# Expert attention in a six-stage decoder: gathered tokens laid out by position, square root on ScalarE, residual by matmul, scores on all partitions

## The reference

```python
probs  = softmax(h @ Wg)                                  # 16 experts
idx    = sort(top_k(probs.T, cap))                        # 2 tokens of each 32 per expert
hg     = h gathered at idx
q, k, v = hg @ Wq[e] + bq, hg @ Wk[e] + bk, hg @ Wv[e] + bv   # 64 features
p      = softmax(q @ k.T / 8, axis=1)                     # over the queries' axis
ao     = (p @ v) @ Wo[e] + bo
y      = h + scatter_add(ao at idx)
yn     = layer_norm(y) * ln_g + ln_b
out    = layer_norm(h + yn)                               # the decoder's own norm
```

## Time and profile before

| what | value |
| --- | --- |
| median of 3 runs | 3803.97 us (3803.84 to 3806.27) |
| profiled execution | 3800.63 us, span 3797.80 us |
| mean granted TensorE clock | 0.95 |
| busy: TensorE, VectorE, ScalarE, GpSimd | 3290, 3118, 2817, 2568 us |

### The profile page before, as it was taken

The page is one execution under the profiler, slowest core; times in us unless marked ns, Lnnn a source line. Parts: engine busy times, 40 slices in busy tenths (PEclk is TensorE's granted clock), DMA queues, the critical chain, the costliest instruction groups (busy, mean ns, idle before and its releaser), DMA issues. The chain is left out here.

```text
span 3797.8 us, 75246 instructions
## 1 busy us (share of the span) xinstructions
PE 3290.3 (87%) x23328; PEld 2494.5 (66%) x23360; DVE 3118.3 (82%) x5163; ACT 2817.2 (74%) x5141; POOL 2567.5 (68%) x2971
## 2 busy tenths in 40 slices
PE   8996988979963688999988989898899879997887
PEld 5664666668542477777767777777777757775565
DVE  5665999955386699999899989989999849998887
ACT  2222777854475799899898998989899737776887
POOL 1222767730086599888888988898898936665676
PEclk9998999979976899999999999999999989998999
DMA  2112222242213111121111211111111112322111
GB/s 61 55 55 56 44 53 49 50 106 46 52 34 85 37 52 57 50 54 53 54 53 56 57 50 57 49 53 56 55 52 51 48 47 68 77 54 64 51 61 45
DMA packets 285549, 209.62 MB, mean 55 GB/s; under 512 B 131416, under 2 KB 249752, under 8 KB 285224
## 3 DMA queue, kind: packets, MB, share of 16 engines
q1 hardware_dynamic: 285224, 205.72, 19.9%
HBM read 149.18 MB, written 51.41 MB: 53 GB/s over the span
## 5 line engine op out<-in xcount | busy, mean ns | idle before, releaser
L2896 POOL TENSOR_TENSOR ma_ch<-ma_h,ma_crep 128x512 f32<-128x512 f32 x1024 | 1348.2, 1340 | 190.5 <-DVE ma_h L3007 159.8
L3007 DVE TENSOR_TENSOR_SCAN ma_h<-ma_a,ma_pbu 128x512 f32<-128x512 f32 x1024 | 1196.5, 1203 | 123.5 <-PE ma_pbu L2576 108.1
L2576 PE MATMUL ma_pbu<-ma_ident,ma_bu 128*128 128x128 f32 x4096 | 655.6, 284 | 120.6 <-DVE ma_h L3007 92.6
L2576 PEld LDWEIGHTS ma_pbu<-ma_ident,ma_bu 128*128 128x128 f32 x4096 | 481.5, 144 | 349.2 <-DVE ma_h L3007 204.3
L2785 ACT ACTIVATE ma_a<-ma_dt,ma_A 128x510 f32<-128x510 f32 x1024 | 672.8, 711 | 1.3 <-issue 1.3
L2585 PE MATMUL ma_py<-ma_ident,ma_ch 128*128 128x128 f32 x4096 | 623.9, 278 | 9.8 <-DVE ma_gT L3025 7.8
L2778 ACT ACTIVATE ma_bu<-ma_uT,ma_b_t 128x512 f32<-128x512 f32 x864 | 555.6, 711 | 13.0 <-PE ma_pbu L2576 11.3
L2585 PEld LDWEIGHTS ma_py<-ma_ident,ma_ch 128*128 128x128 f32 x4096 | 493.4, 145 | 14.3 <-DVE ma_gT L3025 11.4
L1576 POOL TENSOR_TENSOR xa_prob<-xa_e,xa_rec_head 128x616 f32<-128x616 f32 x128 | 155.6, 1217 | 126.4 <-DVE xa_rec_head L1668 114.2
L924 POOL TENSOR_TENSOR xa_prob<-xa_e,xa_rec_head 128x616 f32<-128x616 f32 x128 | 155.7, 1217 | 107.0 <-DVE xa_rec_head L1016 90.4
L362 POOL TENSOR_TENSOR la_veps<-la_mv,la_eps 128x2 f32<-128x2 f32 x32 | 6.3, 196 | 248.8 <-DVE la_mv L395 248.8
(11 more groups left out here) (375 smaller groups left out, 7942.3 us busy)
## 6 DMA issues: line engine op xcount, KB each, us to landing
ma_crep<-ma_ct_dram SPq DMA_DIRECT2D x256, 256.0 KB
xa_x<-act SPq DMA_DIRECT2D x64, 256.0 KB, 2.7
act<-xa_y SPq DMA_DIRECT2D x64, 256.0 KB, 2.2
la_x<-in_x SPq DMA_DIRECT2D x32, 256.0 KB, 2.8
act<-la_y SPq DMA_DIRECT2D x32, 256.0 KB
act<-ea_x SPq DMA_DIRECT2D x32, 256.0 KB, 4.0
ma_x<-act SPq DMA_DIRECT2D x16, 512.0 KB, 4.5
ma_xr<-act SPq DMA_DIRECT2D x16, 512.0 KB
```

The costliest lines, as they stand in the source:

```text
L2576: last = pe.transpose(pbu[c % 2][:, t * P:(t + 1) * P], bu[:, s % 2, t, c * P:(c + 1) * P], ident[:, :])
L2896: pool.tensor_tensor(ch[:, s % 2, c], h[:, s % 2, c], crep[:, s % 4, :], ALU.mult).then_inc(multiplied, 1)
L3007: dve.tensor_tensor_scan(out=h[:, s % 2, c, :], data0=a[:, s % 2, c, :], data1=pbu[c % 2][:, :], initial=0.0, op0=ALU.mult, op1=ALU.add).t ...
```

## The change

- `hg` is laid out by tile, `[P, NT, 64, SP]`: the slots of one tile lie together. Transposes read it directly, and `stage` and `slots` go. The experts read their tokens as runs of 4 positions, one run per tile, and write them back so.
- `sums` is a 128x128 matrix of two blocks of ones, made by VectorE. One score call of 512 columns leaves every score on all 64 partitions of its half, in one of two PSUM buffers. `spread`, `pick` and the scaling of `prob` go; the exponential is done in two calls, and `weigh` multiplies probability, reciprocal sum and value in one instruction per value token.
- The residual is added in PSUM by a product of the identity with `x`, with three banks; the first addition and `r` go, and `moments` and `normalise` read `py`.
- GpSimd's addition and power go. ScalarE takes `Sqrt(var + eps)` into PSUM (`std`), and VectorE takes two reciprocals, one to SBUF (`rstd`) for ScalarE, one to PSUM (`factor`) for its own `shift`.

```diff
-        hg = outer.sb("hg", [P, C * E * 2, S])
+        hg = outer.sb("hg", [P, NT, C * E * 2, SP])
...
-                        act.activation(hg[:, :, 2 * SP * v:2 * SP * (v + 1)],
-                                       pg[v % 2][:, :, :, :, :].rearrange("p c k t s -> p (c k) (t s)"),
+                        act.activation(hg[:, 2 * v:2 * v + 2],
+                                       pg[v % 2][:, :, :, :, :].rearrange("p c k t s -> p t (c k) s"),
...
-                return hg[:, at:at + 2, :]
+                return hg[:, :, at:at + 2, :].rearrange("p t i s -> p i t s")
...
-                    for k in range(2):
-                        last = pe.matmul(pa[:, :], sums[:, k, :], prod[:, e % 2, k, :], start=(k == 0), stop=(k == 1))
-                    last.then_inc(att_made, 1)
-                def spread(e):
...
+                    at_least(pe, exp_done, e - 1)
+                    pe.matmul(pa[e % 2][:, :, :].rearrange("p k s -> p (k s)"), sums[:, :],
+                              prod[:, e % 2].rearrange("p k s -> p (k s)"), start=True, stop=True).then_inc(att_made, 1)
...
-                    act.activation(prob[:, e % 2, :], pa[0:4, :], ACT.Exp, bias=nmax[:, e % 2:e % 2 + 1],
-                                   accum_out=rsum[:, e % 2:e % 2 + 1]).then_inc(exp_done, 1)
+                    for k in range(2):
+                        last = act.activation(prob[:, e % 2, k, :], pa[e % 2][:, k, :], ACT.Exp, bias=nmax[:, e % 2, k:k + 1],
+                                              accum_out=rsum[:, e % 2, k:k + 1])
+                    last.then_inc(exp_done, 1)
...
-                    link(dve.tensor_tensor(pv[:, :, :], pb[:, :, :], v_sb[:, e % 2], ALU.mult))
-                    dve.tensor_tensor(av[:, e % 2, :], pv[:, 0, :], pv[:, 1, :], ALU.add).then_inc(av_ready, 1)
+                    link(dve.reciprocal(rsum[:, q, :], rsum[:, q, :]))
+                    for k in range(2):
+                        last = dve.scalar_tensor_tensor(out=pv[:, k, :], in0=prob[:, q, k, :], scalar=rsum[:, q, k:k + 1],
+                                                        in1=v_sb[:, q, k, :], op0=ALU.mult, op1=ALU.mult)
+                    link(last)
+                    dve.tensor_tensor(av[:, q, :], pv[:, 0, :], pv[:, 1, :], ALU.add).then_inc(av_ready, 1)
...
-            py = [ps(f"py{k}", [P, 2, D]) for k in range(2)]
+            py = [ps(f"py{k}", [P, 2, D]) for k in range(R)]
+            small = ps("small", [P, 2, 2, 4])
+            std, factor = small[:, 0], small[:, 1]
...
-                    pe.wait_ge(turn_copied, k + 1)
-                    at_least(pe, res_added, k - 1)
+                    at_least(pe, z_ready, k - R + 1)
                     for t in range(2):
-                        last = pe.matmul(py[p][:, t, :], turned[:, p, t, C, :],
-                                         turned[:, p, t, 0:C, :].rearrange("p c d -> p (c d)"), start=True, stop=True)
+                        pe.matmul(py[k % R][:, t, :], ident[:, :], x[:, 2 * k + t, :], start=True, stop=False)
+                        if t == 0:
+                            pe.wait_ge(turn_copied, k + 1)
+                        last = pe.matmul(py[k % R][:, t, :], turned[:, p, t, C, :],
+                                         turned[:, p, t, 0:C, :].rearrange("p c d -> p (c d)"), start=False, stop=True)
...
-                def stage(k):
...
+                def deviation(n):
+                    act.wait_ge(var_ready, n + 1)
+                    act.activation(std[:, n % 2, :], mv[:, n % 2, :, 1], ACT.Sqrt, bias=eps[:, 0:1]).then_inc(std_ready, 1)
...
+                act.preload_act_table_set("sqrt_and_others")
...
-                        link(pool.tensor_tensor(veps[:, n % 2, :], mv[:, n % 2, :, 1], eps[:, :], ALU.add))
-                        pool.tensor_tensor(rstd[:, n % 2, :], veps[:, n % 2, :], minus_half[:, :], ALU.pow).then_inc(rstd_ready, 1)
...
-                def first(k):
-                    dve.wait_ge(y_made, k + 1)
-                    at_least(dve, z_ready, k - R + 1)
-                    dve.tensor_tensor(r[:, k % R], py[k % 2][:, :, :], pair_tiles(k), ALU.add).then_inc(res_added, 1)
...
-                        dve.wait_ge(rstd_ready, n + 1)
+                        dve.wait_ge(std_ready, n + 1)
+                        dve.reciprocal(rstd[:, n % 2, :], std[:, n % 2, :])
+                        link(dve.reciprocal(factor[:, n % 2, :], std[:, n % 2, :]))
                         dve.scalar_tensor_tensor(out=shift[:, n % 2, :], in0=mv[:, n % 2, :, 0], scalar=-1.0,
-                                                 in1=rstd[:, n % 2, :], op0=ALU.mult, op1=ALU.mult).then_inc(shift_ready, 1)
+                                                 in1=factor[:, n % 2, :], op0=ALU.mult, op1=ALU.mult).then_inc(shift_ready, 1)
```

More of the change, by code:

```diff
@@ L1990, in expert_attention @@
             pq, pk, pw = ps("pq", [P, S]), ps("pk", [P, 2, S]), ps("pw", [P, 2, S])
-            pa, pb = ps("pa", [P, S]), ps("pb", [P, 2, S])
+            pa = [ps(f"pa{q}", [P, 2, S]) for q in range(2)]
             po = ps("po", [P, 2, C, S])
@@ L2016, in queries @@
                         for i in range(2):
-                            last = pe.matmul(pq[halves[i], :], wq[:, e % WS, c, :], of_expert(c, e)[:, i, :],
+                            last = pe.matmul(pq[halves[i], :], wq[:, e % WS, c, :], of_expert(c, e)[:, i],
                                              start=(c == 0), stop=(c == C - 1))
@@ L2089, in output @@
                     for c in range(C):
[L2090 removed]
+                        last = act.activation(of_expert(c, e), po[:, :, c, :].rearrange("p i (t s) -> p i t s", t=NT), ACT.Identity, bias=bo[:, c:c + 1])
                     last.then_inc(out_copied, 1)
@@ L2117, in products, with largest, weigh @@
                                       ALU.mult).then_inc(prod_ready, 1)
-                def softmax(e):
+                def largest(e):
+                    dve.wait_ge(att_made, e + 1)
+                    dve.tensor_reduce(nmax[:, e % 2, :], pa[e % 2][:, :, :], AX.X, ALU.max, negate=True).then_inc(max_ready, 1)
+                def weigh(e):
                     q = e % 2
-                    dve.wait_ge(att_made, e + 1)
-                    dve.tensor_reduce(nmax[:, q:q + 1], pa[0:4, :], AX.X, ALU.max, negate=True).then_inc(max_ready, 1)
                     dve.wait_ge(exp_done, e + 1)
[L2124 to L2128, removed]
                     dve.wait_ge(v_ready, e + 1)
-                    link(dve.tensor_tensor(pv[:, :, :], pb[:, :, :], v_sb[:, e % 2], ALU.mult))
-                    dve.tensor_tensor(av[:, e % 2, :], pv[:, 0, :], pv[:, 1, :], ALU.add).then_inc(av_ready, 1)
+                    link(dve.reciprocal(rsum[:, q, :], rsum[:, q, :]))
[4 more added lines that the diff above has]
+                    dve.tensor_tensor(av[:, q, :], pv[:, 0, :], pv[:, 1, :], ALU.add).then_inc(av_ready, 1)
                 link = Chain(dve, chain, 0)
+                link(dve.memset(sums[:, :], 0.0))
+                for i in range(2):
+                    last = dve.memset(sums[halves[i], halves[i]], 1.0)
+                last.then_inc(sums_ready, 1)
                 dve.wait_ge(c_loaded, 16 * len(constants))
@@ L2144, in _ @@
                     if e + 1 < E:
-                        softmax(e + 1)
+                        largest(e + 1)
+                        weigh(e + 1)
                     if e + 2 < E:
@@ L2281, in moments @@
                     for t in range(2):
-                        last = dve.bn_stats(stats[:, which, t, :], src[:, t, :])
+                        last = dve.bn_stats(stats[:, n % 2, which, t, :], src[:, t, :])
                     link(last)
```

81 lines of the change are left out of this document (27 added, 54 removed).

## The result

The changed kernel takes 3736.4 us, the median of 4 runs (3731.99 to 3739.45), beside 3803.9 us (4 runs, 3802.32 to 3806.27) before: 0.9821 of it, 95% interval 0.9804 to 0.9838. The profiled execution took 3739.45 us, span 3736.6.

What follows compares the result with a forecast made beforehand. TensorE was taken to bound the experts, GpSimd the scatter, after the change the port it shares with VectorE; 19.4 + 29.6 + 5 = 54 us saved gave 3750 us, range 3738 to 3782.

Steps and rivals of the forecast that it cites:

- 16 experts: Expert stage, bound by TensorE: dropping the spread product (1.06 us) and merging score calls (0.15 us) per expert saves 19.4 us.
- 31 periods of the scatter: Scatter with both layer norms: each pair of tiles falls from 4.26 to 3.13 us, saving 29.6 us over 31 periods.
- tail: End of the scatter, after the last residual addition: four steps save 1.25 us each, 5 us taken, bounds 1 and 6.
- starts of experts, scatter, next stage: Scatter start taken as 0 (range -0.6 to +1.9 us); TensorE's wait for the summing matrix at the experts' start rounded away.
- What both hold in turn is 2.44 + 0.68 = 3.12 us: SBUF port shared by GpSimd and VectorE in the scatter: two GpSimd products plus VectorE's second addition set the pair.
- ScalarE's 3.07 us: ScalarE per scatter pair: 4.26 less staging copy 0.52 and idle 0.92, plus 0.25 for the square root.
- VectorE, 2.98 in the forecast: VectorE per scatter pair: 4.26 less first addition 0.58 and `shift` wait 1.15, plus 0.45 for small operations.
- The 0.15 us of the score call: Experts, TensorE: two 256-column score calls in 1.06 us become one 512-column call of 0.91, saving 0.15 us per expert.
- rival B: Experts: strided token reads slow TensorE; doubled projections and queries add 74 us, giving 3824 us; chance 0.06.
- C: Scatter: TensorE stays partly at half clock and becomes the bound, 3.4 us a pair, 8 us less saved, 3758; chance 0.07.
- D: Scatter hardly gains: chains between engines set the pair at about 3.6 us, 14.6 us less saved, 3765; chance 0.10.
- A: Scatter: VectorE's second addition waits a whole GpSimd product every pair, 4.24 us a pair, no gain there, 3782; chance 0.12.

## Why the forecast was too slow

The direction was right, and so were the engines named as limits: TensorE in the experts, the port in the scatter. The sum was short, term by term:

| term, us saved | forecast | measured |
| --- | --- | --- |
| 16 experts | 19.4 | 17.6 |
| 31 periods of the scatter | 29.6 | 37.2 (1043.80 to 1133.23) |
| tail | 5 | 6.5 |
| starts of experts, scatter, next stage | 0 | -1.9 |
| block | 54 | 59.3 |

**The step that failed** is "What both hold in turn is 2.44 + 0.68 = 3.12 us" and the 3.13 us taken from it. That the port would set the pair was right, the size of its second part was not. 2.44 are start-to-start times, but 0.68 is the length of a record, whose end overlaps the next instruction: start to start the same addition takes 0.57 (1086.47 to 1087.04 in the kernel without bias), which gives 3.01. Measured, GpSimd goes round in 2.92 us with two instructions of 1.22 to 1.23 alone, so the second addition costs it 0.47 us; where the addition fell into a product, it cost 0.46. Why that is less than 0.57 no run shows. The rows shown had a nearer figure: the power lost 0.54 to this addition, not 0.68. The Trainium skill, "SBUF — State Buffer", section "SBUF: two separate sides", lets the one that starts first hold the pair of ports for the whole instruction; by the length of the record that would be 3.12, start to start 3.01, and here the measurement decides.

ScalarE's 3.07 us was too large as well, and the port alone would not have mended the forecast: with 2.92 for the port the largest sum would have been 3.07. ScalarE stands at 2.83: the turned copy takes 0.74 us start to start where the sum had 0.84, the two normalisations 1.89 where it had 1.98, and the root 0.19, not 0.25. VectorE, 2.98 in the forecast, stands at 2.83 too. In steady pairs the difference from 3.13 is 0.21 us each, 6.5 us; the shorter periods at both ends give another 1.1.

**Experts:** the spread was 16 x 1.06 = 17.0 us, as summed; the other 0.6 us lie outside the steady period. The 0.15 us of the score call wasn't there: I took a 512-column call's time from four that follow one another (0.455 us apart), but the two records of the score call keep 0.53 apart. In the steady period no wait for the score chain showed, and no half-rate reads (rival B).

**Starts:** taken as nothing, they cost 1.9 us. The experts begin 0.9 us later: routing ends 0.4 later, and TensorE then waits 2.15 us until the summing matrix is made, where it stood 1.67 before. The scatter's start costs 0.7, the next stage's 0.3. The table's 59.3 us run to the next stage's table load (1211.94 to 1152.64) and so hold the 0.9, which 287.6 less 227.4 leaves out.

**The rivals.** C: granted clock 1.00 through the 31 periods. D: the pair stands only 0.09 us above the next two sums, so chains cost next to nothing. A did not occur after the change, but my reason against it was wrong: that "a late VectorE finds it idle and the phase corrects itself" is refuted by the kernel with the residual on VectorE, where GpSimd idles 1.36 us a pair and the addition still falls into the product. What saved this kernel is the order: the second addition stands ahead of the moments, so it asks at the end of the bias addition. The same page of the Trainium skill, section "Who interferes with whom", says that the order of issue decides who blocks. The two pairs of kernels that differ only in order agree: 2.92 against 3.32 us, 3.53 against 4.30.

**The rest of the miss** isn't in the sum. The forecast for the median stood 13.6 us high: 5.3 from the block, 1.9 from the untouched stages in the two profiles, and 6.4 since I carried over that the median stood 3.3 us above the profiled execution, where it now stands 3.1 below. Any one of the three is more than the 1.6 us by which the time left the range, and the last two are no larger than what runs of one kernel differ by (3731.99 to 3739.45), so that it fell just outside is in part chance. My range had nothing for the level of the other stages.

The parts do not add up: undoing the power costs 1.25 us a pair, the residual 1.38 or 0.61, the staging copy 0.43, for 1.34 gained. Each relieves a different engine, so the pair needs all of them.

## What to carry to other kernels

When two engines share a port, add start-to-start times, take the loss from a pair of rows in which the two met, and ask at which moment the second one asks: the place of one call was worth 0.4 to 0.8 us a pair here with no work added. Sum each engine after the change, not the parts: the maximum decides, and an edit alone may give little. When untouched stages move by ten microseconds and more between runs, as here, read the gain off the edited stretch of the trace and give the range of the total room for the others.

## What was not expected of the hardware

- Records that overlap need not mean a wait: a `shift` with two SBUF operands ran in 0.16 us when it started 0.03 us before GpSimd's next instruction, with no gap between the two of GpSimd; it took 1.22 when it started 0.05 us after one.
- ScalarE's normalisation from PSUM takes 0.56 us in the changed kernel where the one from SBUF takes 0.59 to 0.60 (1.02 and 1.08 for two).
- TensorE reads its moving operand in runs of four fp32, 1 KB apart, at the same 3.63 us for the two projections.
- Code that was not changed ran 13 and 17 us longer behind one edit, in both profiles, with gaps of 5 to 6 us in which VectorE waits for nothing named.
